# Block inverses of a causal layer: layout changes by 32x32 transposes on VectorE instead of transfers through DRAM

## The reference, cut to what matters

```python
hidden_states: (4, 512, 128); 16 heads of 8
logits = einsum('bhqd,bhkd->bhqk', q, k) * scale
probs  = softmax(logits + causal_mask)
L      = eye(s) - tril(probs, -1)
rhs    = diagonal(probs)[..., None] * v
A      = solve_triangular(L, rhs, lower=True)
out    = A.transpose(0, 2, 1, 3).reshape(b, s, HID) @ Wd.T + bd
```

## Time and profile before

| what | value |
|---|---|
| median of three runs | 1425.99 us |
| the profiled execution | 1419.46 us, span 1417.7 us |
| busy share of the span | TensorE 80%, VectorE 70%, ScalarE 48%, GpSimd 44% |
| TensorE's granted clock | 0.886 of full speed |
| the causal layer | about 625 to 1094 us of the span |
| program 0's last copy to program 15's | 742.1 to 1091.7 us |
| STREAM_TRANSPOSE of 128x32, 112 times | 23.9 us on VectorE |
| transfers e_nat to e_scr, xT from x_scr | 128 of 16 KB each |

### The profile page before, as it was taken

The page is one execution under the profiler, slowest core; times in us unless marked ns, Lnnn a source line. Parts: engine busy times, 40 slices in busy tenths (PEclk is TensorE's granted clock), DMA queues, the critical chain, the costliest instruction groups (busy, mean ns, idle before and its releaser), DMA issues. The chain is left out here.

```text
span 1417.7 us, 32912 instructions
## 1 busy us (share of the span) xinstructions
PE 1138.5 (80%) x12875; PEld 622.9 (44%) x12906; DVE 987.3 (70%) x2114; ACT 684.9 (48%) x1412; POOL 630.7 (44%) x838
## 2 busy tenths in 40 slices
PE   6745867769999998853788888988885899999975
PEld 2212322323333334842465666666674233333375
DVE  5699999978888884536936664636511888888453
ACT  3843433424776766521452352443330276776744
POOL 2369979954235312531353352444441623241153
PEclk9879879977999999876888989979978699999988
DMA  5388934132241402244142232241111233140222
GB/s 153 126 298 322 338 117 174 46 80 60 44 107 43 115 2 89 66 104 90 28 90 55 34 81 46 35 106 28 32 21 28 69 76 79 46 132 10 85 57 88
DMA packets 132800, 127.65 MB, mean 90 GB/s; under 512 B 86295, under 2 KB 117847, under 8 KB 128122
## 3 DMA queue, kind: packets, MB, share of 16 engines
q1 hardware_dynamic: 124592, 117.65, 29.6%
q0 software_dynamic: 2496, 5.13, 1.1%
q10 hardware_dynamic: 5558, 2.76, 0.9%
HBM read 104.83 MB, written 37.90 MB: 101 GB/s over the span
## 5 line engine op out<-in xcount | busy, mean ns | idle before, releaser
L1400 DVE TENSOR_REDUCE f_row_min<-f_ps 128x1 f32<-128x512 f32 x512 | 327.5, 681 | 62.5 <-PE f_ps L1720 61.9
L1282 ACT ACTIVATE f_e<-f_ps 128x512 f32<-128x512 f32 x512 | 278.6, 598 | 124.0 <-PE f_ps L1739 118.7
L1720 PE MATMUL f_ps<-f_operands 72*128 72x512 bf16 x512 | 204.1, 409 | 19.9 <-DMA f_operands<-k_scr 14.5
L1739 PE MATMUL f_ps<-f_operands 75*128 75x512 bf16 x512 | 189.9, 381 | 2.6 <-ACT f_e L1282 1.6
L790 PE MATMUL m_ps<-m_shared,sb_ident 128*128 128x512 f32 x256 | 134.3, 672 | 59.8 <-DVE m_shared L630 59.8
L363 POOL TENSOR_TENSOR m_drive<-m_du,m_ring 128x1024 f32<-128x1024 f32 x64 | 149.6, 2349 | 55.0 <-DVE m_ps L622 36.5
L495 ACT ACTIVATE m_ps<-m_delta,m_A 128x511 f32<-128x511 f32 x128 | 83.0, 681 | 131.5 <-DVE m_ps L622 109.0
L1750 PE MATMUL f_ps<-f_e,f_v_op 128*32 128x512 f32 x1024 | 137.3, 608 | 2.4 <-ACT f_e L1282 1.4
L2546 DVE TENSOR_REDUCE d_row_min<-d_ps 128x1 f32<-128x384 f32 (+3 forms) x176 | 104.6, 632 | 27.2 <-PE d_ps L2769 26.3
L1720 PEld LDWEIGHTS f_ps<-f_operands 72*128 72x128 bf16 x512 | 51.2, 100 | 161.9 <-DVE f_row_min L1400 110.4
L790 PEld LDWEIGHTS m_ps<-m_shared,sb_ident 128*128 128x128 f32 x256 | 52.1, 214 | 144.1 <-DVE m_shared L630 88.5
(11 more groups left out here) (297 smaller groups left out, 2168.7 us busy)
## 6 DMA issues: line engine op xcount, KB each, us to landing
m_ring<-bc_scr SPq DMA_DIRECT2D x32, 1024.0 KB, 5.5
f_rows_scr<-blank SPq DMA_DIRECT2D x2, 8707.5 KB, 31.0
f_wall<-f_wall SPq DMA_DIRECT2D x16, 578.0 KB
f_operands<-q_scr SPq DMA_DIRECT2D x32, 288.0 KB
f_operands<-k_scr SPq DMA_DIRECT2D x96, 96.0 KB
d_q_op<-q_scr SPq DMA_DIRECT2D x12, 288.0 KB
d_k_op<-k_scr SPq DMA_DIRECT2D x36, 96.0 KB
f_operands<-f_rows_scr SPq DMA_DIRECT2D x46, 64.5 KB, 1.8
```

The source lines that it names most:

```text
L1282: nc.scalar.activation(e_sb[:, n % 3, hh, :], ps[:, SCORE[(b * UNITS + u) % SCORE_BANKS], :], ACT.Exp, scale=SCALE).then_inc(s["e_out"], 1)
L1400: nc.vector.tensor_reduce(row_min[:, b % 2, u // TPB, u % TPB:u % TPB + 1], ps[:, MAXQ[(b * UNITS + u) % MAX_BANKS], :], AX.X, ALU.max, ne ...
L1720: nc.tensor.matmul(ps[:, MAXQ[n % MAX_BANKS], :], q_op(b, QK)[:, hd, t * P:(t + 1) * P], k_op(b, QK)[:, hd, :], start=True, stop=True).the ...
L1739: nc.tensor.matmul(ps[:, SCORE[n % SCORE_BANKS], :], k_op(b, QKS)[:, hd, t * P:(t + 1) * P], q_op(b, QKS)[:, hd, :], start=True, stop=True ...
```

## The change: what it does

The two DRAM buffers, `blocks_out` and `inverses` are gone. VectorE takes over both changes of layout:

- `block_turned(n, r)`, for r from 0 to 3: one transpose of 32 partitions by 512 elements. For the span r of 32 tokens it reads the span's own 32 columns of all heads of `e_nat`, in sixteen groups of 32 (2 blocks x 16 heads; the heads are 512 bytes apart), and transposes each group. Both blocks' columns come out for both blocks' rows.
- `halves_joined(n)`: one 128x256 operation that takes the right half for each partition and writes `e_blk`, with the inner axes already swapped.
- `inverse_turned(n, r)`: one transpose of 32 partitions by 512 elements from `xz` to the diagonal of `xT`; it writes the heads 512 bytes apart.
- `z_half`, a 128x32 multiplication behind the reciprocal of `inverted_sums`; GpSimd's last scaling writes 128x512 instead of 128x256, with zeros outside the partition's own block, and strided; its first reads `e_blk` straight.

The places are fixed by new functions. `block_turned` stands at the four hooks that follow the last diagonal scores of tile m in the hook order, `halves_joined` one hook later: at hooks 0 to 3 and 4 of program m - 2 if m % 4 is 0, at 6 to 9 and 10 of program m - 3 if it is 1 (and for tile 2), at 4 to 7 and 8 of program m - 3 for the others. Tile 0 has all five at hook 13 of program -3. `inverse_turned(m, r)` stands at hooks 5 to 8 of program m - 1; tile 0's four at hook 2 of program -1. For tile 0 `multiplied` moves to hooks 3 to 6.

```diff
+MT_HOOKS_FIRST = (3, 4, 5, 6)
+        def gathered_at(m, r):
+            return (-3, 13) if m == 0 else hooks_after(own_scores_end(m), 1 + r)
+        def blocks_turned_at(m):
+            return (-3, 13) if m == 0 else hooks_after(own_scores_end(m), 1 + SPANS)
+        def spread_out_at(m, r):
+            return (-1, 2) if m == 0 else (m - 1, 5 + r)
 (GpSimd)
-                    pool.wait_ge(s["e_in"], 16 * (n + 1))
-                    nc.gpsimd.tensor_tensor(xT_blk[:, :, :], e_blk[:, :, :].rearrange("p i c -> p c i"),
+                    pool.wait_ge(s["e_in"], n + 1)
+                    nc.gpsimd.tensor_tensor(xT_blk[:, :, :], e_blk[:, :, :],
...
+                    pool.wait_ge(s["z_half"], n + 1)
                     if n >= 1:
-                        pool.wait_ge(s["x_stored"], 16 * n)
-                    nc.gpsimd.tensor_tensor(xz_blk[:, :, :], xT_blk[:, :, :],
-                                            zi_blk[:, :].unsqueeze(2).to_broadcast([P, BLK, BLK]),
+                        pool.wait_ge(s["x_in"], SPANS * n)
+                    nc.gpsimd.tensor_tensor(xz[:, :, :, :].rearrange("p i a c -> p a c i"),
+                                            xT_blk[:, :, :].unsqueeze(1).to_broadcast([P, 2, BLK, BLK]),
+                                            z_half[:, :, :].unsqueeze(3).to_broadcast([P, 2, BLK, BLK]),
 (SyncE: blocks_out, inverses and their calls taken out)
 (VectorE)
+                    nc.vector.tensor_tensor(z_half[:, :, :], zi_blk[:, :].unsqueeze(1).to_broadcast([P, 2, BLK]),
+                                            w["half"].unsqueeze(2).to_broadcast([P, 2, BLK]), ALU.mult)
+                def block_turned(n, r):
+                    own = slice(r * SPAN, (r + 1) * SPAN)
+                    if r == 0:
+                        dve.wait_ge(s["act_out"], own_block_scores(n))
+                        if n >= 1:
+                            dve.wait_ge(s["e_in"], n)
+                    nc.vector.transpose(diagT[own, :, :, :].rearrange("p j a i -> p (j a i)"),
+                                        e_nat[own, n % 3, :, own].rearrange("p h (a j) -> p j a h", a=2))
+                def halves_joined(n):
+                    nc.vector.scalar_tensor_tensor(out=e_blk[:, :, :], in0=diagT[:, :, 1, :], scalar=w["half"][:, 1:2],
+                                                   in1=diagT[:, :, 0, :], op0=ALU.mult, op1=ALU.add)
+                def inverse_turned(n, r):
+                    own = slice(r * SPAN, (r + 1) * SPAN)
+                    if r == 0:
+                        dve.wait_ge(s["blk_step"], BLK_STEPS * (n + 1))
...
+                    nc.vector.transpose(xT[own, n % 2, :, own].rearrange("p h (a i) -> p i a h", a=2),
+                                        xz[own, :, :, :].rearrange("p i a c -> p (i a c)"))
 (TensorE, multiplied)
-                        pe.wait_ge(s["x_in"], 16 * BLKS * (n + 1))
+                        pe.wait_ge(s["x_in"], SPANS * (n + 1))
```

More of the change, by code:

```diff
@@ L123, in lay_out @@
         "blocks": np.kron(np.eye(BLKS), np.ones((BLK, NH))).astype(np.float32),
+        "half": np.stack([np.arange(P) % SPAN < BLK, np.arange(P) % SPAN >= BLK], axis=1).astype(np.float32),
         "in_block": np.tile(np.eye(BLK, dtype=np.float32), (BLKS, 1)),
@@ L1924, in delta_phase @@
     q_scr, k_scr = core.q_scr, core.k_scr
-    e_scr, x_scr = core.e_scr, core.x_scr
     with ExitStack() as ctx:
@@ L1965, in delta_phase @@
         xT_blk = sb("xT_blk", [P, BLK, BLK])
-        xz_blk = sb("xz_blk", [P, BLK, BLK])
+        z_half = sb("z_half", [P, 2, BLK])
+        diagT = sb("diagT", [P, BLK, 2, BLK])
+        xz = sb("xz", [P, BLK, 2, BLK])
         xT = sb("xT", [P, 2, NH, P])
@@ L2073, in block_sums_in, with mt_in @@
             return []
+        def mt_in(n, h):
+            hooks = MT_HOOKS_FIRST if n == -1 else MT_HOOKS
+            return hooks.index(h) if in_program(n + 1) and h in hooks else None
         def scores_in(n, h):
@@ L2088, in scores_in, with own_scores_end, hooks_after @@
             return list(range(each * (h - 2), min(each * (h - 1), GROUPS_OF[t]))) if h >= 2 else []
+        def own_scores_end(m):
+            return next((m - 3, h) for h in range(HOOKS) if DIAG_GROUPS - 1 in scores_in(m - 3, h))
+        def hooks_after(place, more):
+            return place[0] + (place[1] + more) // HOOKS, (place[1] + more) % HOOKS
+        def gathered_at(m, r):
[4 more added lines that the diff above has]
+            return (-1, 2) if m == 0 else (m - 1, 5 + r)
         def values_at(b):
@@ L2116, in later_tile_at, with quarters_at, block_work_at @@
             return m if m is not None and m % TPB else None
+        def quarters_at(place, n, h):
+            return [(m, r) for m in range(n + 1, n + 4) if in_program(m) for r in range(SPANS) if place(m, r) == (n, h)]
+        def block_work_at(place, n, h):
+            return next((m for m in range(n + 1, n + 4) if in_program(m) and place(m) == (n, h)), None)
         def begins_early(n):
@@ L2158, in delta_phase @@
                     act_use("score", n + 3, i)
-                if in_program(n + 1) and h in MT_HOOKS:
-                    act_use("mt", n + 1, MT_HOOKS.index(h))
+                if mt_in(n, h) is not None:
+                    act_use("mt", n + 1, mt_in(n, h))
                 if later_tile_at(sums_at, n, h) is not None:
@@ L2308, in _ @@
                 for n in range(-LEAD, TILES_N):
-                    if n == -1:
-                        sp.wait_ge(s["zero_set"], 2)
-                    if in_program(n + 1):
-                        inverses(n + 1)
-                    if in_program(n + 3) and (n + 3) % TPB != 0:
-                        blocks_out(n + 3)
                     if in_program(n + 3) and (n + 3) % TPB == 0:
@@ L2325, in _ @@
                         first_queries()
-                    if in_program(n + 3) and (n + 3) % TPB == 0:
-                        blocks_out(n + 3)
                 sp.wait_ge(s["parts_stored"], 16 * 2 * PARTS * (B + 1))
@@ L2421, in beside @@
                         exponential(n + 3, i)
-                    if in_program(n + 1) and h in MT_HOOKS:
-                        multiplied(n + 1, MT_HOOKS.index(h))
+                    if mt_in(n, h) is not None:
+                        multiplied(n + 1, mt_in(n, h))
                     if goes_on(n, 4) is not None:
@@ L2634, in beside @@
                         inverted_sums(m)
+                    for m, r in quarters_at(spread_out_at, n, h):
+                        inverse_turned(m, r)
                     m = maxima_done(n, h)
@@ L2651, in beside @@
                         spread_sums(m)
+                    for m, r in quarters_at(gathered_at, n, h):
+                        block_turned(m, r)
+                    m = block_work_at(blocks_turned_at, n, h)
+                    if m is not None:
+                        halves_joined(m)
                     b = goes_on(n, LEAD)
@@ L3003, in build @@
         core.y_scr = nc.dram_tensor("y_scr", [T + REGION_ROWS, H], F32, kind="Internal").ap()
-        core.e_scr = nc.dram_tensor("e_scr", [TILES, BLKS, NH, BLK, BLK], F32, kind="Internal").ap()
-        core.x_scr = nc.dram_tensor("x_scr", [TILES, BLKS, NH, BLK, BLK], F32, kind="Internal").ap()
         core.bc_scr = nc.dram_tensor("bc_scr", [B, 2 * N_STATE, S], F32, kind="Internal").ap()
```

37 lines of the change are left out of this document (16 added, 21 removed).

## The result

The changed kernel takes 1534.49 us (median of 4 runs, 1527.77 to 1540.44) against 1425.52 for the kernel before on the same chip (4 runs): ratio 1.0765, 95% interval 1.0722 to 1.0808. The direction was as forecast, the size was not: +109 us, where +54 stood, and outside the range of 1446 to 1522. The profiled execution took 1535.15 us, its span 1533.4.

A forecast was written before the change was run, and what follows sets the result against it. The prediction took TensorE as the bound by busy sums, but VectorE as setting the pace before turn 5 in some programs. Its terms by program summed to +54 us, giving 1480 us, range 1446 to 1522.

The forecast's parts named there:

- What bounds the kernel: TensorE by busy sums, but VectorE sets the pace up to turn 5 in program 7; place counts, not the sum.
- The price of a transpose: Each new 32x512 transpose on VectorE takes 0.70 us; lower end 0.60, upper end 1.03 if strides cost.
- The overlap between quadrants: Three of four new transposes and their followers on VectorE lose 0.08 us of overlap, about 9 us over 128.
- Programs with n % 4 = 3: Programs 3, 7, 11: 6.2 us of new VectorE work before turn 5, 0.36 idle; +5.8 us each, +17.4.
- n % 4 = 2: Programs 2, 6, 10: 9.4 us of new VectorE work, idle 0.52 + 1.38; +7.5 us each, +22.5.
- n % 4 = 1: Programs 1, 5, 9: four transposes at hooks 5 to 8 and `z_half`, 3.0 us; +2.0 us each, +6.0.
- n % 4 = 0: Programs 0, 4, 8: 6.2 us of work at hooks 4 to 8 against 5.3 us idle; +0.4 us each, +1.2.
- Programs 12 to 15: No maxima there: 16 transposes find room and the 2.65 us wait for xT in program 14 goes; -2.65 us.
- Filling: Programs -3 to -1: 12.9 us of new VectorE work, less 2.1 idle and 1.3 credited for earlier `multiplied`; +9.5 us.
- Strides cost: Rival: each transpose takes 1.03 us, 42 us more on VectorE, about 34 of it counting; 1514 us, chance 0.14.
- The clock falls: Rival: waiting for VectorE lowers TensorE's clock in nine programs with maxima, +16 us; 1496 us, chance 0.12.
- The spare time takes it all: Rival: VectorE's idle time absorbs the new work and only removed waits count, 9.8 us; 1416 us, chance 0.08.

The follow-up runs named there:

- micro: VectorE alone, trains of independent 512-element operations, not the kernel: a 512-byte step costs about 0.64 ns per element, changing quadrants a pitch of 0.73 us against 0.60.
- dense: The changed kernel with its 32x512 transposes reading and writing without strides (the wrong elements): 1504.03 us, ratio 1.0543 to the kernel before.
- q0: The changed kernel with all new transposes beginning at partition 0, strides kept: 1509.45 us, ratio 1.0579 to the kernel before.
- loaded: The kernel before, transfers kept, plus equal transposes and additions on VectorE at the changed kernel's places, which nobody waits for: 1535.70 us, ratio 1.0765.
- tiny_early: The changed kernel with transposes of 32x32 instead of 32x512 for tiles 0 to 2 alone: 1515.20 us, ratio 1.0640 to the kernel before.
- bare: The changed kernel with one 32x32 transpose for each train of four and a join of 128x16: 1419.18 us, ratio 0.9978 to the kernel before.
- warm12: The changed kernel with twelve matmuls, their result overwritten, before TensorE's wait for xT of tiles 1 to 15: 1541.02 us, ratio 1.0819 to the kernel before.
- moved: The changed kernel with most block_turned at hooks 0 and 1 and inverse_turned of tiles 1 to 15 at hook 13, both in program m - 2: 1513.82 us.
- spread_moved: The changed kernel with only inverse_turned of tiles 1 to 15 moved, to hooks 0 and 1 of program m - 1: 1514.63 us, ratio 1.0643.

## Why the prediction was right and wrong, step by step

- **What bounds the kernel** (VectorE up to turn 5 where n % 4 is 2 or 3): right. These six programs took 67.5 of the 116.4 us, the three of kind 1 8.7; kind 0 grew little, as forecast.
- **The price of a transpose, 0.70 us: the step that failed.** It is 1.04 us, and 1.06 of the path in program 7; "transposes near 1 us" was one of the signs that I had given for being wrong. I had both ends in hand and went to the wrong one. For a dense read spoke L2593 against L2587, 165 and 170 ns. But those have 16 elements, and 0.64 ns for each of 16 is 10 ns, which such rows can't show. GpSimd's L2216 has 256 elements and showed it: the same instruction went from 892 to 730 ns when the change made its read dense, 0.63 ns for each element, the very figure that micro gives for VectorE. My upper end of 1.03 us was right to a hundredth. In time: 30 us (dense).
- **The overlap between quadrants, "0.78 instead of 0.70, about 9 us": mis-sized.** In micro the pitch rises by 0.13 us, 16 us for 128. Besides, an instruction behind the last transpose of a train, which goes back to partition 0, is held too. q0 gave 25 us. This is the rule of the Trainium skill (VectorE: DVE Perf Modes, section "Two Vector instructions with no wait between them"), that such an instruction starts only when all earlier ones have finished; the trains of 8.77 and 3.67 us agree with it. So does program 7: the maxima start at 991.81, 0.16 us before the end of the transpose in front of them, which is at partition 0, and turn 3 at 994.16, 0.03 us after the end of one that is not. In the steady part both a transpose off partition 0 and what follows it are held, about six instructions per train; an estimate of 0.13 us for each in 32 trains is 25 us. I had read the rule and named the neighbours, but charged 0.08 us for some 110 instructions, and then taken 0.70 all the same.
- **The join, 0.42 us:** measured 0.54, 16 x 0.12 = 2 us. Why was not tried: joins of the same shape take 0.45 us in loaded and 0.54 in dense. `z_half` 0.19: right.
- **Programs with n % 4 = 3, +5.8 each:** measured 11.3, 10.5, 10.1. With my own terms and 1.06, 0.54 and 0.19: 8 x 1.06 + 0.73 - 0.36 = 8.9.
- **n % 4 = 2, +7.5 each:** measured 11.4, 13.5, 10.7. Repriced: 12 x 1.06 + 1.08 + 0.19 - 1.9 = 12.1.
- **n % 4 = 1, +2.0 each:** measured 1.1, 3.9, 3.7; repriced 4.4 - 1.0 = 3.4.
- **n % 4 = 0, +0.4 each:** programs 4 and 8 grew by 0.3 and 2.1; program 0 by some 8 (below).
- **Programs 12 to 15, -2.65:** wrong in sign, +2.8, +3.4, +0.2 and +0.9. The wait for the transfer in program 14 went; that transposes of 1.04 us took its place before the turns is likely and was not tried.
- **Filling, +9.5: the second term that failed.** At the values' row of batch 1 VectorE is 22.6 us later (718.35, now 740.96), 1.6 of which it brings from before the layer; tiny_early shows 19 us for all of tiles 0 to 2. Repriced my sum gives 16 x 1.06 + 1.62 + 0.38 - 2.1 - 1.3 = 15.6. The rest, some 5 us, these terms don't have. TensorE, too, stood still here: it waits 7.24 and 6.50 us for the split shifts, which are queued behind the transposes, and 6.10 behind the train of four at hook 2:

```profile
702.17 0.30 PE L2816 MATMUL d_ps<-sb_ident_b,d_min_part 128*48 128x128 bf16 x1 [7.24 <-DVE d_min_part L2573]
...
713.38 0.61 PE L2808 MATMUL d_ps<-d_k_op,d_q_op 96*128 96x512 bf16 x1 [6.10 <-DVE d_row_min L2549]
```

```profile
695.00:720.00 25.00, 10.59 (x102) 5.89 (x105) 24.17 (x54) 3.70 (x10) 0.69 (x1) 0.59 0.01 1
```

  In the same stretch as the earlier trace rows VectorE is busy for 24.2 of 25 us and TensorE for 10.6, where it was 19.6.
- **SyncE's fewer transfers at nothing, GpSimd at nothing:** right in sum (bare), though program 0 has a stall I hadn't thought of. In the middle of one hop's 32 matmuls TensorE waits for nothing but its own instructions:

```profile
765.42 0.54 PE L2962 MATMUL d_ps<-d_mT,d_a_hop 32*32 32x32 f32 x23
770.59 0.33 PE L2962 MATMUL d_ps<-d_mT,d_a_hop 32*32 32x32 f32 x9 [4.63 <-issue]
```

  The kernel before has it at the same instruction, with 2.22 us; in both cases packets of the instruction queues and the next sequence's operands move in that stretch. Why it is longer now was not tried. The stalls of over 0.8 us don't sum to more in the changed kernel (4.6 us, before 10.3), so in sum they aren't part of the loss.
- **The end of program 0, at nothing:** from the values' row to the last copy 31.6 us, before 23.8. The stall is 2.4 us longer, TensorE waits 2.1 us for `xT`, and the same 522 matmuls take 22.8 us instead of 19.0, at a granted clock of 0.72 instead of 0.93.
- **The sum.** At the measured prices my terms give 26.6 + 36.3 + 10.2 for the programs of kinds 3, 2 and 1 and 15.6 for the filling, 88.7 of the 116.4 us. The rest are terms that I had at next to nothing: program 0 (7.9), programs 12 to 15 (7.4), the filling (7.0, with the 1.6 from before the layer), kind 3 (5.3), programs 4 and 8 (2.4), less 2.3 in kinds 1 and 2.
- **The rivals.** "Strides cost" (1514 us, given 0.14) was the true one of them, and it too was 20 us too low; it left the quadrants (25 us) and the filling as they were. "The clock falls" came true beside it: `multiplied` took 54.2 us before and 64.5 after, and in the layer the same 9004 recorded matmuls keep TensorE busy for 397.3 us at a granted clock of 0.75 (625 to 1210 us), before for 365.3 at 0.84 (625 to 1092). It follows from VectorE's delays, as it comes back to 0.876 in bare, and is part of the 109 us, by at most these 32; warm12 can't divide them. "The spare time takes it all" needed turn 5 to be on time; moved and spread_moved show that even at the borders the spare time is mostly a wait before a link.

What stays open: how much of the 109 us goes through the lower clock (at most 32), and how the last 5 us of the filling divide between clock and waits.

```profile
L2830 PE MATMUL d_ps<-d_xT,d_e_nat 128*32 128x112 f32 (+3 forms) x2048 | 54.2, 256 | 15.6 <-DMA d_xT<-x_scr 9.8 <-issue 3.9 <-ACT d_e_off L2394 1.9
```

(the row of the kernel before to which L2872 answers.)
